# Staging the first feed-forward block's weights over two DMA queues, with its first input tiles loaded ahead

## The reference, cut to what matters

```python
x = x + mamba(layernorm(x))
wg = w_gate / 127; wu = w_up / 127; wd = w_down / 127      # int32 in memory, 3072 x 1024 each
h = silu(x_norm @ wg.T) * (x_norm @ wu.T)                  # x_norm = layernorm(x)
x = x + h @ wd.T
```

## Time and profile before

| | us |
|---|---|
| profiled execution, device time | 3330.5 |
| its span on the slowest core (core 4) | 3328.9 |
| spans of the 8 cores | 3291.9 to 3328.9 |
| two timed runs | 3318.2 and 3510.9 (median 3414.5) |

### The profile page before, as it was taken

One profiled execution on the slowest core, in us unless ns is written; L12 is line 12 of the kernel. 1 busy time (PEld: TensorE's weight loads), 2 busy tenths in 40 slices (PEclk: granted clock), 3 DMA queues, 4 the chain that ended last, 5 costly groups with the idle time before them and its releaser, 6 DMA issues.

```text
span 3328.9 us, 29917 instructions; the slowest of 8 cores (3291.9 to 3328.9 us)
## 1 busy us (share of the span) xinstructions
PE 1994.2 (60%) x9274; PEld 975.4 (29%) x9432; DVE 969.8 (29%) x1633; ACT 753.2 (23%) x1180; POOL 323.2 (10%) x404
## 2 busy tenths in 40 slices
PE   0355555555555530474866769415986676768697
PEld 0233333333333310231422324112443333323242
DVE  3244444434444441011212111253442122112110
ACT  0244545445454421200101101010010201101010
POOL 0222322222221210012000000000000000000000
PEclk9677676676766755797888889757998798888887
DMA  7200000000000018525021120343033311120303
GB/s 249 75 13 26 1 26 1 26 26 1 26 1 26 23 48 265 179 87 173 13 73 54 43 85 23 129 155 101 31 116 109 135 53 61 42 85 19 108 0 98
DMA packets 69851, 233.31 MB, mean 70 GB/s; under 512 B 8450, under 2 KB 8578, under 8 KB 67652
## 3 DMA queue, kind: packets, MB, share of 16 engines
q10 hardware_dynamic: 35712, 112.21, 9.8%
q1 hardware_dynamic: 27460, 91.92, 9.0%
q0 software_dynamic: 6528, 27.27, 2.0%
HBM read 170.55 MB, written 60.82 MB: 70 GB/s over the span
## 4 chain that ended last, share of the span: by engine, by line
PE 39%; DMA 21%; DVE 12%; ACT 9%; issue 8%; DVEq 4%; POOLq 2%; POOL 2%; ACTq 2%; SPq 0%
PE ps_s L985 16%; DMA arena<-wd_c 7%; PE ps_s L951 5%; DMA arena<-xs 4%; DVEq L143 4%; PE ps_s L1055 3%; PE ps L1055 3%; POOLq L143 2%; ACT L679 2%; POOL arena L560 2%; PE ps_s L1307 2%; DVE arena L516 2%; PE ps L759 2%; PE ps_s L1233 2%; DMA arena<-wu_t 2%
## 5 line engine op out<-in xcount | busy, mean ns | idle before, releaser
L985 PE MATMUL ps_s<-arena 128*128 128x512 bf16 x2256 | 519.2, 392 | 11.0 <-DVE arena L328 8.6
L584 PE MATMUL ps_s<-arena 128*128 128x256 bf16 x1024 | 212.1, 395 | 341.5 <-ACT arena L508 338.8
L318 PE MATMUL ps<-arena 128*128 128x128 bf16 x512 | 63.5, 307 | 484.8 <-DVE arena L307 484.8
L985 PEld LDWEIGHTS ps_s<-arena 128*128 128x128 bf16 x2304 | 230.7, 100 | 298.0 <-issue 71.7
L1055 PE MATMUL ps_s<-arena 128*128 128x512 bf16 x752 | 212.1, 403 | 136.5 <-DMA arena<-wd_c 85.7
L266 ACT ACTIVATE arena<-arena 128x1024 bf16<-128x1024 f32 x64 | 67.6, 1057 | 908.0 <-DMA arena<-xs 818.0
L584 PEld LDWEIGHTS ps_s<-arena 128*128 128x128 bf16 x1024 | 136.2, 137 | 410.0 <-issue 358.2
L951 PE MATMUL ps_s<-arena 128*128 128x512 bf16 x752 | 171.5, 389 | 118.8 <-DVE arena L906 58.6
L499 PE MATMUL ps_s<-arena 128*128 128x256 bf16 x1024 | 169.6, 338 | 110.2 <-DVE arena L447 62.1
L1000 DVE TENSOR_TENSOR arena<-arena,ps_s 128x512 bf16<-128x512 f32 x144 | 99.0, 688 | 435.3 <-ACT arena L994 435.3
L1055 PE MATMUL ps<-arena 128*128 128x512 bf16 x752 | 214.1, 407 | 0.9
(11 more groups left out here) (94 smaller groups left out, 2335.1 us busy)
## 6 DMA issues: line engine op xcount, KB each, us to landing
xs<-arena ACTq DMA_DIRECT2D x48, 512.0 KB, 2.9
arena<-xs ACTq DMA_DIRECT2D x48, 512.0 KB, 4.6
arena<-wd_c SPq DMA_DIRECT2D x84, 256.0 KB, 2.6
arena<-wd_c ACTq DMA_DIRECT2D x84, 256.0 KB, 2.6
arena<-wg_t SPq DMA_DIRECT2D x16, 768.0 KB, 6.2
arena<-wu_t SPq DMA_DIRECT2D x16, 768.0 KB, 6.8
arena<-x ACTq DMA_DIRECT2D x16, 512.0 KB, 4.0
arena<-w_in ACTq DMA_DIRECT2D x8, 1024.0 KB, 10.1
```

What stands on the lines that cost most here:

```text
L318: lambda e, s=xn_bf_tile, dj=dj, pbf=pbf: e.transpose(pbf[:, dj * P:(dj + 1) * P], s[:, dj * P:(dj + 1) * P], g_ident),
L584: lambda e, dj=dj, ci=ci, bkx=bkx, half=half, par=par: e.matmul(psb[bkx][:, half * TCM:(half + 1) * TCM], win_bf[:, dj * 4096 + ci * P: dj ...
L985: lambda e, hi=hi, dj=dj, bk=bk, par=par, wsrc=wsrc: e.matmul(psb[bk], wsrc[:, dj * H + hi * P: dj * H + (hi + 1) * P], fxnt[par][:, dj * ...
```

## The change

- `F_STG2` moves to 55296, next to slot 0 in `win_bf`, so slot 1 is free after `mk_xz_last` as well. Both slots' loads now wait only for that; the first `wu` conversion waits for the end of Mamba in their place.
- Slot 0's loads stay on SP; slot 1's are issued from POOL's queue.
- ACT makes all 32 conversions; DVE makes none. The cache writes are issued from ACT, right behind the second conversion of each pair.
- The four tiles of chunk 0 (rows 0 to 511 of `xs1`, stored by Mamba's chunks 0 and 1, which get semaphores of their own) are loaded in `emit_ffn1_preamble`, appended to ACT's queue behind Mamba's chunk 6: tiles 2 and 3 into fxB, tiles 0 and 1 into fxA. The layer norm of chunk 0 waits for these alone.
- Chunk 1's first two tiles, whose buffers fxB now hold chunk 0's tiles 2 and 3, wait for chunk 0's stores rather than for the cache writes.

```diff
-F_STG2 = 118784
+F_STG2 = 55296
...
+        def emit_ffn1_preamble():
+            mk_m01 = [(sd_m0, 32), (sd_m1, 32)]
+            for i in range(2):
+                mk = dma("scalar", fxB_g[i][:],
+                         xs1[(2 + i) * P:(3 + i) * P, :], sd_sm,
+                         wait=[mk_xz_last] + mk_m01)
+            for i in range(2):
+                mk = dma("scalar", fxA_g[i][:],
+                         xs1[i * P:(1 + i) * P, :], sd_sm,
+                         wait=[mk_xpe_k[7], mk_r_hist[(7, 7)]] + mk_m01)
+            return {"mk_loads": mk}
...
+            if k == NKM - 2 and N_SUBLAYERS >= 2:
+                ffn1_pre.update(emit_ffn1_preamble())
...
                             if first and c == 1:
-                                w += mk_cache_all
+                                w.append(mk_fst_chunk[0])
...
-                            w = list(mkreg)
-                            if slot == 1:
-                                w += region["wu"]
+                            w = list(region["wg"])
...
-                            mkd = dma("sync", stg[slot][:],
+                            mkd = dma("sync" if slot == 0 else "gpsimd",
+                                      stg[slot][:],
...
-                            if slot == 0:
-                                em.op("scalar",
-                                      ... e.copy(...)
-                                prev2[slot] = s_se.mark()
-                            else:
-                                em.op("vector",
-                                      ... e.tensor_copy(...)
-                                prev2[slot] = s_ve.mark()
-                            mkk[dj] = prev2[slot]
+                            cw = [mkd]
+                            if m == 1 and dj == 0 and hh == 0:
+                                cw += region["wu"]
+                            em.op("scalar",
+                                  ... e.copy(...)
+                                  wait=cw, inc=[(s_se, 1)], drain=False)
+                            prev2[slot] = mkk[dj] = s_se.mark()
...
-                        em.op("gpsimd",
+                        em.op("scalar",
                               ... e.dma_start(cache[...], dstw[...])
-                              wait=[mkk[dj]], inc=[(sd_cache, 16)])
+                              wait=[mkk[dj]], inc=[(sd_cache, 16)],
+                              drain=False)
```

More of the change, by code:

```diff
@@ L243, in build_nc @@
         sd_stq = Sem(ctx.enter_context(nc.semaphore("sd_stq")))
+        sd_stg = Sem(ctx.enter_context(nc.semaphore("sd_stg")))
+        sd_m0 = Sem(ctx.enter_context(nc.semaphore("sd_m0")))
+        sd_m1 = Sem(ctx.enter_context(nc.semaphore("sd_m1")))
         sd_x = [sd_xa, sd_xb]
@@ L305, in ln_norm @@
                     first=True):
+            ew = extra_wait if isinstance(extra_wait, list) else [extra_wait]
             em.op("vector", lambda e, d=dst_bf, s=src_tile, j=col:
@@ L309, in ln_norm @@
                                   op0=ALU.mult, op1=ALU.add),
-                  wait=[mk_stats, extra_wait], inc=[(s_ve, 1)], drain=first)
+                  wait=[mk_stats] + ew, inc=[(s_ve, 1)], drain=first)
             col_free[col] = s_ve.mark()
@@ L752, in mamba_tail @@
             ev0 = s_ve.mark()
+            st_sem = sd_m0 if k == 0 else (sd_m1 if k == 1 else sd_st[par])
             mk_store[k] = dma("scalar",
                               dst1[(k * NTM) * P:(k * NTM + 1) * P, :],
-                              xin[par * 2][:], sd_st[par], wait=[ev0])
+                              xin[par * 2][:], st_sem, wait=[ev0])
             for ci in range(NCI):
@@ L777, in mamba_tail @@
                               dst1[(k * NTM + 1) * P:(k * NTM + 2) * P, :],
-                              xin[par * 2 + 1][:], sd_st[par], wait=[ev1])
+                              xin[par * 2 + 1][:], st_sem, wait=[ev1])
             mk_cevax[par] = mk_store[k]
@@ L788, in build_nc @@
         mamba_transpose(1, [mk_xpe_k[0], mk_xpe_k[0]])
+        ffn1_pre = {}
+        fxA_g = [VA(F_XIN2 + i * 4096, 4096, F32) for i in range(2)]
+        fxB_g = [VA(F_XINB + i * 4096, 4096, F32) for i in range(2)]
+        def emit_ffn1_preamble():
[9 more added lines that the diff above has]
+            return {"mk_loads": mk}
         for k in range(NKM):
@@ L810, in build_nc, with ffn @@
         mk_mamba_stb = sd_stb.mark()
-        def ffn(src, dst, first, region, store_mark_fn):
+        def ffn(src, dst, first, region, store_mark_fn, pre=None):
             wg_bf = VA(F_WG, 49152, BF16)
@@ L819, in fxt @@
             def fxt(c, tt):
+                if pre and c == 0 and tt >= 2:
+                    return fxB[tt - 2]
                 if c % 2 == 1 and tt < 2:
@@ L839, in f_ln_tiles @@
                 tiles = [fxt(c, tt) for tt in tts]
[L840 to L845, removed]
-                        else:
-                            w.append(mk_fst_chunk[c - 2])
-                        if first and c == 1:
-                            w += mk_cache_all
-                    else:
[L851 to L857, removed]
+                if pre and c == 0:
+                    mk_x = pre["mk_loads"]
+                else:
+                    for i, tt in enumerate(tts):
+                        gtile = c * NTF + tt
+                        w = list(store_mark_fn(gtile))
+                        if tt < 2:
+                            if c <= 1:
+                                w += region["xin"]
+                            else:
+                                w.append(mk_fst_chunk[c - 2])
+                            if first and c == 1:
+                                w.append(mk_fst_chunk[0])
+                        else:
+                            if c == 0:
+                                w += region["xin"]
+                            else:
+                                w.append(mk_fst_chunk[c - 1])
+                        mk_x = dma("scalar", tiles[i][:],
+                                   src[gtile * P:(gtile + 1) * P, :],
+                                   sd_x[c % 2], wait=w)
                 mst = ln_stats_group([t[:] for t in tiles], col0, [mk_x])
@@ L860, in f_ln_tiles @@
                     col = col0 + i
+                    ew = trdone.get(("f", tt % 2))
+                    if pre and c == 0 and i == 0 and tts[0] == 0:
+                        ew = [mk_mamba_pe_end, mk_mamba_gp_end,
+                              mk_mamba_ve_end, ew]
                     mkn = ln_norm(fxn[tt % 2][:], tiles[i][:], col, mst,
-                                  trdone.get(("f", tt % 2)),
-                                  first=(i == 0))
+                                  ew, first=(i == 0))
                     bank = 4 + tt % 2
@@ L912, in ffn @@
-                            mkk[dj] = prev2[slot]
+                                      sd_wa if slot == 0 else sd_stg, wait=w)
+                            cw = [mkd]
+                            if m == 1 and dj == 0 and hh == 0:
+                                cw += region["wu"]
+                            em.op("scalar",
+                                  lambda e, dj=dj, hh=hh, dstw=dstw, slot=slot: e.copy(
+                                      dstw[:, dj * H + hh * 1536: dj * H + (hh + 1) * 1536],
+                                      stg[slot][:]),
+                                  wait=cw, inc=[(s_se, 1)], drain=False)
```

16 lines of the change are left out of this document (3 added, 13 removed).

## The result

| | before | changed |
|---|---|---|
| median of all timed runs, us | 3374.4 (11 runs) | 3343.8 (12 runs) |
| lowest, us | 3315.9 | 3335.2 |
| profiled execution, us | 3330.5 | 3342.1 |
| ratio, changed to before | | 1.0080, interval 1.0047 to 1.0113 |

The two medians can't be set against each other: in part of the executions, of either kernel, one die runs at a lower clock; the ratio leaves these out. So the change costs 0.8%, 16 to 37 us, with 27 us as the middle. It is slower, by less than the 2% that I took for the limit of what can be told.

A forecast was written before the change was run, and what follows sets the result against it. The prediction saw 150 us of almost idle PE, with staging rounds hanging on loads, conversions and DMA gaps; +17.5 (earlier start, longer rounds), +0.3 and +0.5 made +18.3 on 3330.5, so 3349 us, range 3300 to 3372.

The forecast's parts named there:

- Tiles loaded ahead: Between Mamba and staging: layer norm no longer waits for Mamba's stores and loads; it and the first conversion come 10.5 us earlier.
- The preamble's cost in Mamba: Four tile loads issued on ACT before Mamba's chunk 7 just fit; cost 0.3 us, at worst 2.
- Rounds of 10.0 us: Staging: a round of two loads and a cache write lengthens from 8.25 to a mean of 10.0 us; first Silu +17.5.
- The conversions in pairs and the DMA share: Signs in the staging: two conversions back to back each round, DMA share about 0.7 rather than 0.85.
- equal sharing between the queues: Staging: loads on two queues share the DMA engines equally and land together; likeliest case, chance 0.5.
- The size of the standstill: Staging: after paired landings nothing moves for 1.47 + 0.1 + 1.8 us, 3.4 us a round, besides three 2.34 us transfers.
- Rival 1: Staging: loads stay staggered and rounds keep 8.25 us; 3322.6 us in all, chance 0.33.
- Chunk 0 to chunk 1: Border of chunks 0 and 1: first two tiles wait for chunk 0's stores; costs 0.5 us, between -1 and +3.
- The total: Whole kernel: +17.5 staging, +0.3 Mamba, +0.5 chunk border, together +18.3 us, giving 3348.8.
- the level it was set on: Base of the sum: profiled execution, 3330.5 us, 84 below the two runs' median (3414.5) and 12 above the lower one.
- within 2%, 0.94: Whole kernel: chance 0.94 of a time within 2% (66 us) of before; faster 0.01, slower 0.05.
- rival 1 or 2: The second, in staging: several queues fill the gaps, rounds fall to the 7.0 us floor; 3303.8 us, chance 0.08.

The follow-up runs named there:

- e4_hw_queue: Changed kernel with slot 1's loads on ACT's queue, behind the cache write, instead of POOL's: round 8.8 us, ratio to before 0.9997.
- e8_defer_cache: Changed kernel with the 16 cache writes moved behind the whole staging, onto POOL's queue: round 6.9 us, ratio to before 0.9904.
- e12_cache_on_sp: Changed kernel with cache writes issued from SP's queue instead of ACT's: round 10.4 us, ratio to before 1.0032.
- e1_one_queue: Changed kernel with slot 1's loads issued from SP's queue again, so both slots' loads share one queue: round 8.8 us, ratio to before 0.9996.

## Why the prediction was right or wrong

- **Tiles loaded ahead: right.** 10.5 us forecast; Mamba's end to first conversion fell from 26.6 to 16.0 us on core 4, 10.3 in the median of the cores. The preamble's cost in Mamba does not show: from the end of the issue of chunk 6's stores to the next ACT instruction it is 3.9 us in both kernels (1156.2 to 1160.1 before, 1162.8 to 1166.7 with the four tile loads between).
- **Rounds of 10.0 us: right in size.** Slot 1's conversions start between 1245.8 and 1398.1, 10.16 us a round; 10.3 over the cores. ACT turns to the first Silu at 1400.2, which is 20.0 us later against Mamba's end than before, where I had 17.5. The conversions in pairs and the DMA share (0.64; I had named 0.7) came as written.
- **The step that failed: equal sharing between the queues.** I wrote that what is under way on two queues shares the DMA engines, and that this makes the loads land together. e4_hw_queue has two queues and they don't; e8_defer_cache has the very queues of the change, without the write, and they don't either. In all kernels here it took POOL's queue and the cache write together. The trace of the changed kernel shows what happens in place of the sharing. In the round in which the write is issued at 1339.11, slot 1's load at 1339.60 (POOL) and slot 0's at 1341.09 (SP), these are the packets and MB of each queue (q10 is ACT's, q0 POOL's, q1 SP's), first from 1339.8 to 1341.8 us, then from 1341.8 to 1347.8:

```profile
q10 hardware_dynamic: 128, 0.79, 98.3%
```
```profile
q0 software_dynamic: 143, 0.79, 45.6%
q1 hardware_dynamic: 141, 0.79, 35.4%
q10 hardware_dynamic: 16, 0.00, 0.1%
```

  The write moves alone and whole. POOL's load has its first packet 2.6 us after its issue (1.2 us in e8_defer_cache, from 1278.8 to 1280.0), so most of its lead over SP's load is lost, and then the two loads share and land together. The rounds of 1289 and 1319 us show the same, and one of e12_cache_on_sp. The earlier trace rows had shown only the queues of SP and ACT beside each other; the jump from them to POOL's queue beside a write had no row.
- **The size of the standstill.** I had 3.4 us; it is 2.7 to 3.0, and the rest of the 10.16 us, 7.2 to 7.5, goes to the three transfers, for which I had 7.0. The two errors met at nearly the right sum, so that the 10.0 was in part luck.
- **A misread page.** I put the DMA line's 8 and 5 into slices 15 and 16, beside PE's 3 and 0. In the earlier trace rows they stand in slices 16 and 17, and slice 15 has a 1. No term uses this.
- **Rival 1 and the skill's rule.** The rule of the Trainium skill ("DMA: Bandwidth & Descriptors", "Issuing engines are not separate DMA queues") holds for e4_hw_queue, 8.8 us on two queues as on one. It does not hold for POOL's queue beside a write, where spreading cost 1.5 us a round, and where the write and POOL's load did not interleave.
- **Chunk 0 to chunk 1: right.** From the last eviction (1591.9) to the layer norm (1601.8) 10.0 us, against 9.0: +0.9, with 0.5 forecast.

```profile
1589.40 2.47 DVE L1095 SCALAR_TENSOR_TENSOR arena<-ps,arena 128x512 f32<-128x512 f32 x4
1601.84 2.35 DVE L278 TENSOR_REDUCE arena<-arena 128x1 f32<-128x1024 f32 x2 [9.96 <-DMA arena<-xs]
```

- **The total, and the level it was set on: the second step that failed.** +18.3 us forecast; chunk 1 starts 20.8 us later against Mamba's end, and the runs say 27 (16 to 37). That 3349 lies 5 us above the measured median is partly luck, since the level was wrong. I built the sum on the profiled execution, 3330.5. The kernel's usual level, 3316 to 3325 us in five of the eleven runs above, is 5 to 15 us below it, and the median shown, 3414.5, was 84 above. Beside that median the forecast of 3349 reads as a gain, while its own sum says a loss. And I took 2% for what a measurement can tell. It told 0.8% with 0.3 to either side, so "within 2%, 0.94" gave away the direction that the sum had: slower, unless rival 1 or 2 held.

**What stays open.** Why a load on POOL's queue has to wait for the write. Its issue comes 0.5 us after the conversion and takes 0.53, where SP needs 0.1 and 0.33, so it goes out behind the write's. With one queue (e1_one_queue) slot 1's load and the write are both issued at 1275.47, the load's first packet comes at 1276.4, ahead of the write's at 1277.4, and the two share. Whether a load on SP's queue that is issued half a microsecond later would wait as POOL's does was not tried, so lateness and the queue itself are not parted. In the changed kernel POOL's loads are issued 1.5 us ahead of slot 0's (1289.64 and 1291.14) and land with them: 7.8 and 8.1 us in the medians of `wg_t` and `wu_t` against 6.4 and 6.7. Without writes the same loads land in 4.6. Nor is it known which part of the effect would remain without the drains.

## What to carry to other kernels

Two buffers that are emptied by one engine are only fast if their loads land apart; look for a stretch in which that engine works and the DMA share is 0.00. Before loads are spread over queues, give them more buffers, and take out of the stage every transfer that nobody in it needs: here two more buffers gained some 32 us and, with four buffers, writes moved behind the staging 18 more at the start of chunk 1 (28 by the ratios), at unchanged work, while POOL's queue for half of the loads lost 21 (28 by the ratios). An operation is moved in time by what it waits for, not by its place in a queue that is otherwise empty.

## What the runs showed of the hardware

The rate within one round of the changed kernel, a microsecond at a time:

```profile
1290.20:1291.20 1.00, 0.00 (x0) 0.00 (x0) 0.00 (x0) 0.86 (x1) 0.00 (x0) 0.50 1.03 430
1291.20:1292.20 1.00, 0.00 (x0) 0.00 (x0) 0.00 (x0) 0.00 (x0) 0.00 (x0) 0.50 0.84 283
1292.20:1293.20 1.00, 0.00 (x0) 0.00 (x0) 0.00 (x0) 0.00 (x0) 0.00 (x0) 0.50 0.86 190
1294.20:1295.20 1.00, 0.00 (x0) 0.00 (x0) 0.00 (x0) 0.00 (x0) 0.00 (x0) 0.50 1.00 412
```

The write is issued at 1289.17, the loads at 1289.64 and 1291.14. The first line is the write alone, 430 GB/s; the last is loads only, 412 GB/s. Between them, where the write ends and the loads begin, it is 283 and 190 GB/s, with the DMA engines hardly less busy (0.84 and 0.86). A dip shows at the same place in e12_cache_on_sp (184 GB/s at a share of 1.00) and in e4_hw_queue (215 at 0.80). So my single 2.34 us a piece was an average of quite different rates. It may be part of why moving the writes out of the rounds shortened them by 3.4 us (10.3 to 6.9) rather than by 2.3; that the loads then no longer land together is another part. That a mixture of reads and writes is the cause was not tried by itself.
